# Batch 2's shared network behind the last mix, two thirds of batch 3's behind the expert loop

## The reference

```python
# x (4, 512, 512), ctx (4, 512, 256)
q = ctx @ Wq.T + bq;  k = ctx @ Wk.T + bk            # (4, 512, 128)
attention = softmax(q @ k.T, axis=-1)
x = x + tanh(g_xattn) * (layernorm(x) @ attention.T)
h = layernorm(x).reshape(-1, 512)
shared = (sigmoid(h @ shared_gate.T) * (h @ shared_up.T)) @ shared_down.T
weights = softmax(h @ router_w.T);  top_w, top_idx = top_k(weights, 2)
# routed: bfloat16, sum over the two chosen experts e of a token
routed = top_w * ((sigmoid(h @ w_gate[e].T) * (h @ w_up[e].T)) @ w_down[e].T)
x = x + tanh(g_ffn) * (h + shared + routed)
```

## Time and profile before

| what | us |
|---|---|
| median of three runs (lowest, highest) | 332.44 (330.88, 333.1) |
| the profiled execution | 332.47 |
| its span, first to last event | 330.7 |
| TensorE busy | 295.4 |
| VectorE, POOL, ScalarE busy | 216.4, 158.8, 132.0 |
| mean granted clock of TensorE | 0.973 of full |

### The profile page before, as it was taken

The page is one execution under the profiler, slowest core; times in us unless marked ns, Lnnn a source line. Parts: engine busy times, 40 slices in busy tenths (PEclk is TensorE's granted clock), DMA queues, the critical chain, the costliest instruction groups (busy, mean ns, idle before and its releaser), DMA issues.

```text
span 330.7 us, 6138 instructions
## 1 busy us (share of the span) xinstructions
PE 295.4 (89%) x1596; PEld 208.7 (63%) x1608; DVE 216.4 (65%) x585; ACT 132.0 (40%) x235; POOL 158.8 (48%) x238
## 2 busy tenths in 40 slices
PE   7579789999999999999999998799999999997280
PEld 2247658786878776877887786566666666663120
DVE  0788878478756588745467488576777676775291
ACT  2263577606657406678104370134343434342000
POOL 3706892685701757402767046035565555565100
PEclk9999989999999999999999999999999999999587
DMA  7999699022060120000159994333434334339499
GB/s 247 342 229 319 98 210 291 27 96 79 20 237 0 50 80 0 0 4 0 64 116 210 208 207 154 83 89 121 124 100 110 113 97 126 98 99 314 134 316 343
DMA packets 30612, 45.91 MB, mean 139 GB/s; under 512 B 3008, under 2 KB 20160, under 8 KB 30592
## 3 DMA queue, kind: packets, MB, share of 16 engines
q1 hardware_dynamic: 20016, 27.66, 27.5%
q0 software_dynamic: 10432, 17.99, 22.9%
q10 hardware_dynamic: 144, 0.00, 0.0%
HBM read 39.58 MB, written 14.72 MB: 164 GB/s over the span
## 4 chain that ended last, share of the span: by engine, by line
PE 68%; DMA 7%; DVE 7%; POOL 7%; issue 6%; ACT 2%; SPq 1%; POOLq 0%; DVEq 0%; ACTq 0%
PE bank L677 13%; PE bank L472 11%; PE bank L473 11%; PE bank L474 11%; PE bank L694 7%; POOL xg L398 5%; PE bank L484 4%; PE bank L467 4%; PE bank L669 3%; PE bank L685 2%; DMA z<-ysb,desti 2%; DMA zb<-z 2%; DMA wqk_sb<-wqk 1%; DVE acc L1272 1%; DVE prob L951 1%
## 5 line engine op out<-in xcount | busy, mean ns | idle before, releaser
L888 ACT ACTIVATE sigc<-bank 128x352 f32<-128x352 f32 x39 | 18.1, 463 | 67.0 <-PE bank L677 67.0
L451 POOL DMA_INDIRECT z<-ysb,desti x36 | 36.1, 1002 | 9.6 <-issue 9.3
L472 PE MATMUL bank<-lnT_hi,sgu_lo 128*128 128x512 f32 (+2 forms) x96 | 39.1, 407 | 1.6 <-DVE lnT_lo L988 1.6
L473 PE MATMUL bank<-lnT_lo,sgu_hi 128*128 128x512 f32 (+2 forms) x96 | 37.8, 394 | 0.0
L474 PE MATMUL bank<-lnT_hi,sgu_hi 128*128 128x512 f32 (+2 forms) x96 | 37.8, 394 | 0.0
L398 POOL DMA_INDIRECT xg<-lnb,slot x32 | 31.9, 996 | 9.9 <-issue 7.6
L1239 DVE TENSOR_TENSOR hrow<-sigc,bank 128x352 bf16<-128x352 f32 x39 | 20.3, 521 | 24.3 <-ACT sigc L888 16.9
L677 PE MATMUL bank<-wgu_lo,xTb 128*128 x156 | 36.0, 313 | 0.0
L677 PE MATMUL bank<-wgu_hi,xTb 128*128 x156 | 36.0, 312 | 0.0
L387 POOL TENSOR_TENSOR hT_lo<-sig,hT_hi 128x512 fp32r<-128x512 f32 (+1 forms) x9 | 11.6, 1289 | 45.7 <-ACT hT_hi L800 45.7
L1245 DVE TENSOR_SCALAR ysb<-bank,wt 128x512 bf16<-128x512 f32 x39 | 29.1, 747 | 5.7 <-DMA z<-ysb,desti 2.8
(11 more groups left out here) (178 smaller groups left out, 651.1 us busy)
## 6 DMA issues: line engine op xcount, KB each, us to landing
xt<-xg SPq DMA_DIRECT2D x39, 129.0 KB
xT_raw<-xT SPq DMA_DIRECT2D x4, 1024.0 KB, 7.3
acc<-x SPq DMA_DIRECT2D x4, 1024.0 KB, 9.5
out<-acc SPq DMA_DIRECT2D x16, 256.0 KB, 3.5
wgu_lo<-wguT POOLq DMA_DIRECT2D x2, 1408.0 KB, 13.3
wgu_hi<-wguT POOLq DMA_DIRECT2D x2, 1408.0 KB, 13.3
cx<-ctxT SPq DMA_DIRECT2D x4, 512.0 KB, 4.3
wd_sb<-wdT POOLq DMA_DIRECT2D x2, 1024.0 KB
```

Source lines behind the costliest of these rows:

```text
L451: nc.gpsimd.indirect_dma_start(out=z, out_offset=bass.IndirectOffsetOnAxis(ap=desti[:, r:r + 1], axis=0), in_=ysb[:, r, :], in_offset=None ...
L472: pe.matmul(dst, a_lo, b_hi, start=first, stop=False)
L473: pe.matmul(dst, a_hi, b_lo, start=False, stop=False)
L888: act.activation(sigc[:, v, :], bank[2 * v][:, 0:I], ACT.Sigmoid).then_inc(s["csig"], 1)
```

## The change

Batches 0 and 1 keep their order. For batches 2 and 3 each engine's list is written anew. On TensorE: project(3) and the energies of batch 3 are woven into mix(2); the turns of its softmax come earlier; mix(3) stands behind rank(2), in the middle of batch 2's shared network, whose rest and whose down product stand behind mix(3). Batch 3 gets only slice 0 of its shared network (with the logits) ahead of the loop; its lnT takes the space of probT. Slices 1 and 2 and the down product go behind the loop, the down product of a token tile into one bank with its two z rows. za and zb have room for all 16 tiles; zb is loaded in 8 pairs up front, and stores follow. tanh(g_ffn) is no longer in the routing weights but in the last addition. Buffers and banks are placed anew for it. wgu_hi and wd_sb are issued behind scatter(2) and factors2(3). The diff of the parts that the prediction speaks of:

```diff
+            for i in range(NB):
+                sp.dma_start(za[:, LT * i:LT * (i + 1)], zt[0, :, LT * i:LT * (i + 1)]).then_inc(s_za[i], 16)
+            sp.wait_ge(s["cy"], NE)
             for r in range(SLOTS):
                 sp.wait_ge(s_yd[r], 16 * len(range(r, NE, SLOTS)))
-
-            def store(t):
-                sp.wait_ge(s["comb"], t + 1)
+            for i in range(0, TT, 2):
+                sp.dma_start(zb[:, i:i + 2], zt[1, :, i:i + 2]).then_inc(s_zb[i // 2], 16)
+            for t in range(TT):
+                if t < LT * last_b:
+                    sp.wait_ge(s["comb"], t + 1)
+                else:
+                    sp.wait_ge(s["shared"], t + 1)
                 sp.dma_start(out[t * P:(t + 1) * P, :], acc[:, t, :]).then_inc(s["outd"], 16)
-            for t in range(TT):
-                if t >= ZS:
-                    store(t - ZS)
-                sp.dma_start(zb[:, t % ZS], zt[1, :, t]).then_inc(s_zl[t % ZS], 16)
-            for t in range(TT - ZS, TT):
-                store(t)
             sp.wait_ge(s["outd"], 16 * TT)
...
+            b = last_b - 1
+            x_low(last_b)
+            factors2(b)
+            factor1(last_b)
+            rows_copy(b)
+            scatter(b, 0)
+            scatter(b, 1)
+            factors2(last_b)
+
+            pool.wait_ge(s["eng"], TT)
+            pool.wait_ge(s["xmm"], TT)
+            for k in range(KP, NT):
+                pool.dma_start(wgu_hi[:, k - KP], wguT[:, k * P:(k + 1) * P, :].rearrange("e p i -> p e i")).then_inc(s["wgu2_in"], 16)
+            for k in range(IT):
+                pool.dma_start(wd_sb[0:KI[k], k], wdT[:, k * P:k * P + KI[k], :].rearrange("e p n -> p e n")).then_inc(s["wd_in"], 16)
+            rows_copy(last_b)
+            scatter(last_b, 0)
+            scatter(last_b, 1)
...
@@ -515,52 +554,71 @@
 
             def turn_ln2(b, j):
                 pe.wait_ge(s["ln2"], LT * b + j + 1)
-                if j >= 2:
+                if j >= 2 and b != last_b - 1:
                     pe.wait_ge(s["lnTlo"], LT * b + j - 1)
+                elif j >= 2:
+                    pe.wait_ge(s["lnTlo"], LT * b + j - 1)
+                elif b == last_b:
+                    pe.wait_ge(*((s["lgshift"], 2 * b), (s["place"], b))[j])
...
+                    pe.wait_ge(s_zb[t // 2], 16)
+                    pe.matmul(bank[6 + j % 2][:, :], identb[:], za[:, t, :], start=True, stop=False)
+                    pe.matmul(bank[6 + j % 2][:, :], identb[:], zb[:, t, :], start=False, stop=False)
                 for c in parts:
                     pe.wait_ge(s["hlo"], IT * b + c + 1)
                     k = ORDER[c]
                     m = KI[k]
                     mm = three(bank[6 + j % 2][:, :], hT_hi[0:m, k, tok], hT_lo[0:m, k, tok],
-                               sd_hi[0:m, k, :], sd_lo[0:m, k, :], c == 0, c == IT - 1)
+                               sd_hi[0:m, k, :], sd_lo[0:m, k, :], c == 0 and b < last_b, c == IT - 1)
                 if parts[-1] == IT - 1:
                     mm.then_inc(s["dm"], 1)
...
+            b = last_b - 1
+            project(last_b, 0)
+            project(last_b, 1)
+            mix(b, range(0, 1))
+            energy(last_b, 0)
+            energy(last_b, 1)
+            mix(b, range(1, 2))
+            energy(last_b, 2)
+            mix(b, range(2, 3))
+            energy(last_b, 3)
+            mix(b, range(3, 4))
+            down(b - 1, 0)
+            turn_prob(last_b, 0)
+            turn_prob(last_b, 1)
+            down(b - 1, 1)
+            turn_ln2(b, 0)
+            turn_ln2(b, 1)
+            down(b - 1, 2)
+            turn_ln2(b, 2)
+            turn_ln2(b, 3)
+            down(b - 1, 3)
+            wide_shared(b, 0, 1)
+            turn_prob(last_b, 2)
+            turn_prob(last_b, 3)
+            wide_shared(b, 0, 0, range(0, 2))
+            turn_logits(b)
+            wide_shared(b, 0, 0, range(2, NT))
+            wide_shared(b, 1, 0)
+            rank(b)
+            mix(last_b)
+            wide_shared(b, 1, 1, range(0, 2))
+            turn_ln2(last_b, 0)
+            turn_ln2(last_b, 1)
+            wide_shared(b, 1, 1, range(2, NT))
+            turn_ln2(last_b, 2)
+            turn_ln2(last_b, 3)
+            wide_shared(b, 2, 0)
+            wide_shared(last_b, 0, 1)
+            wide_shared(b, 2, 1, range(0, 2))
+            turn_logits(last_b)
+            wide_shared(b, 2, 1, range(2, NT))
+            wide_shared(last_b, 0, 0)
+            rank(last_b)
+            for j in range(LT):
+                down(b, j)
...
+            wide_shared(last_b, 1, 0)
+            wide_shared(last_b, 1, 1)
+            wide_shared(last_b, 2, 0)
+            pe.wait_ge(s["hid"], IT * last_b + 2)
+            for t in range(4):
+                routed(t)
+            wide_shared(last_b, 2, 1)
+            for t in range(4, 8):
+                routed(t)
+            down(last_b, 0)
+            for t in range(8, 10):
+                routed(t)
+            down(last_b, 1)
+            for t in range(10, 12):
+                routed(t)
+            down(last_b, 2)
+            down(last_b, 3)
 
...
+            b = last_b - 1
+            qk(last_b)
+            act.activation(warm[:], less_mean[:], ACT.Exp)
+            for j in range(LT):
+                soft(last_b, j)
+            for j in range(LT):
+                normalise(last_b, j)
+            prob_high(last_b, 0)
+            prob_high(last_b, 1)
+            x_high(last_b)
+            for j in range(LT):
+                ln2_high(b, j)
+            rows_again(b)
+            logits_out(b)
+            prob_high(last_b, 2)
+            prob_high(last_b, 3)
+            choice_exp(b)
+            gate_shared(b, 0)
+            for j in range(LT):
+                add_ln2(b, j)
+            hidden_high(b, 0)
+            gate_shared(b, 1)
+            ln2_high(last_b, 0)
+            ln2_high(last_b, 1)
+            hidden_high(b, 1)
+            ln2_high(last_b, 2)
+            ln2_high(last_b, 3)
+            gate_shared(b, 2)
+            rows_again(last_b)
+            logits_out(last_b)
+            act.activation(warm[:], less_mean[:], ACT.Exp)
+            hidden_high(b, 2)
+            choice_exp(last_b)
+            gate_shared(last_b, 0)
+            for j in range(LT):
+                add_ln2(last_b, j)
+            hidden_high(last_b, 0)
 
...
+            b = last_b - 1
+            qk_low(last_b)
+            residual(b, range(0, 1))
+            row_max(last_b, 0)
+            row_max(last_b, 1)
+            residual(b, range(1, 2))
+            row_max(last_b, 2)
+            over_sum(last_b, 0)
+            over_sum(last_b, 1)
+            residual(b, range(2, 3))
+            row_max(last_b, 3)
+            over_sum(last_b, 2)
+            over_sum(last_b, 3)
+            residual(b, range(3, 4))
+            ln2_apply(b)
+            prob_low(last_b, 0)
+            shared_out(b - 1, 0)
+            prob_low(last_b, 1)
+            ln2_low(b, 0)
+            shared_out(b - 1, 1)
+            ln2_low(b, 1)
+            ln2_low(b, 2)
+            shared_out(b - 1, 2)
+            ln2_low(b, 3)
+            shared_out(b - 1, 3)
+            prob_low(last_b, 2)
+            prob_low(last_b, 3)
+            choose(b)
+            weights(b)
+            places(b)
+            shared_hidden(b, 0)
+            residual(last_b, range(0, 2))
+            hidden_low(b, 0)
+            residual(last_b, range(2, LT))
+            ln2_apply(last_b)
+            shared_hidden(b, 1)
+            ln2_low(last_b, 0)
+            ln2_low(last_b, 1)
+            hidden_low(b, 1)
+            ln2_low(last_b, 2)
+            ln2_low(last_b, 3)
+            choose(last_b)
+            shared_hidden(b, 2)
+            hidden_low(b, 2)
+            weights(last_b)
+            places(last_b)
+            dve.wait_ge(s["rowsb"], NB)
+            dve.wait_ge(s["rowsb2"], NB)
+            tables_tiles()
+            tables_limits()
             tables_rows()
...
+            shared_hidden(last_b, 1)
+            for r in range(SLOTS):
+                dve.wait_ge(s_yd[r], 16 * len(range(r, NE, SLOTS)))
+            hidden_low(last_b, 1)
+            for t in range(4):
+                add_routed(t)
+            shared_hidden(last_b, 2)
+            add_routed(4)
+            add_routed(5)
+            hidden_low(last_b, 2)
+            for t in range(6, 8):
+                add_routed(t)
+            add_routed(8)
+            add_routed(9)
+            shared_out(last_b, 0)
+            add_routed(10)
+            add_routed(11)
+            shared_out(last_b, 1)
+            shared_out(last_b, 2)
+            shared_out(last_b, 3)
```

More of the change, by code:

```diff
@@ L537, in rank @@
                 sel = picked[:].rearrange("p j e -> p (j e)")
[L538 to L543 removed]
+                pe.matmul(rank_bank(b)[:, 0:LT * E], tri[:], sel, start=True, stop=True)
```

(5 more changed lines are left out.)

336 lines of the change are left out of this document (174 added, 162 removed).

## The result

The changed kernel takes 345.84 us (median of 4 runs, 344.86 to 347.6); the kernel before took 332.77 beside it (4 runs, 330.88 to 333.45). The ratio is 1.041, 95% interval 1.035 to 1.047: 13.1 us slower, where 13.2 was forecast. The profiled execution took 345.78 (span 344.0).

The account below looks back on a forecast made before the run. TensorE was taken as the bound, busy 295.4 of 330.7 us. Slots 4.6, clock 1.4, 1.7 and 2.1, and tail 3.4 sum to 13.2 on a median of 332.44: 345.7 us, range 340 to 353.

Parts of the forecast that it names:

- Step 1: Batch 2: TensorE idle 9.9 us before its first turn of lnr2, as rstd2 queues behind x_low(3) on POOL.
- Step 2: Batch 3: POOL and VectorE queues leave TensorE idle 3.4 and 1.4 us; its scatters start 4.6 us later.
- Step 3: Lower clock behind TensorE's idle times: 1.4 us after 9.9 idle, 1.7 after 3.4, 2.1 in the expert loop.
- the first wait: TensorE's idle time of 9.9 us in batch 2, with 1.4 us priced for the lower clock behind it.
- The weights: wgu_hi and wd_sb, issued later, all there at 211.0, ahead of the loop's start at 219.2: costed at nothing.
- Step 4: Tail behind the expert loop: 84 matmuls came and the gap holds 36, so 3.4 us longer.
- The rule weighed: x_low on POOL gets shorter with VectorE nearly idle: estimate 4.3 us, making the sum 345.4.

Follow-up runs that it names:

- e1: Changed kernel with x_low(3) on POOL behind factors2(2) and factor1(3) instead of ahead of them: 336.42 us, ratio 1.012 to the kernel before.
- e2: Changed kernel with x_high(3) on ScalarE ahead of batch 3's four normalisations instead of behind prob_high(3,1): 343.13 us, ratio 1.030 to the kernel before.
- e3: Changed kernel with all twelve matmuls of up product wide_shared(2,1,1) ahead of turn_ln2(3,0), not six ahead and six behind turn_ln2(3,1): 346.46 us, ratio 1.041.
- e5: Changed kernel with 24 and 26 matmuls on unread data filling TensorE's idle time ahead of the expert loop: 343.4 us, ratio 1.028 to the kernel before.
- e8: e3 with the two loads of wgu_hi issued on POOL ahead of batch 2's scatters instead of behind factors2(3): 346.3 us, ratio 1.043.
- e4: Changed kernel with one matmul instead of three in every product of batch 3 behind the expert loop: 341.64 us, ratio 1.027 to the kernel before.

## Why the prediction was right, step by step

**Step 1** held: the wait stood where the chain put it, 9.43 us for 9.9. x_low took 4.49 us for the 4.60 taken. e1 and e2 moved the turn by 8.0 and 3.7 us when the wait was taken away in whole and in part, and with the whole of it 7.5 of the 13.2 us at the end went.

**Step 2** held: the slots came 7.6 us later in the rows (201.25 against 193.63), for 4.6 + 1.4 + 1.7 = 7.7, and the places on the way held too: the first turn of batch 3's rows at 178.63 (177.2 and 1.4 of clock) and the third at 184.27 (181.0 and 3.1). e3 took 1.9 us of its idle time away and moved the slots by 0.7.

**Step 3** was right in what happens and a little off in a size: against the kernel before the loop lost 1.5 us to the clock, not 2.1; e5 gave back 1.7 in the loop. The 1.4 behind the first wait were there (0.50 in 144.34 to 148.00), but they are not the price of a long idle time: e1, with 1.42 and 0.63, paid them too.

**The weights** are the term that failed. They were all there when the prediction had them, at 211.6 (forecast 211.0), but "Costed at nothing; the scatters hide it" compared this with the loop's start. What counts is the scatters, which POOL issues behind them and which land behind them. From slots to the first wide product it took 19.19 us, not 17.87: 1.3 us, and e8 brought back 17.83. In e4, with the same order, it was 0.5, so that this size rests on single executions.

**Step 4** held, 0.5 too high: the tail is 2.85 us longer, not 3.4; e4 showed that its products make it so.

So 7.6 + 1.3 + 1.5 + 2.9 = 13.3 stands where 13.2 was forecast: a term of 1.3 that was missing and two that were 0.6 and 0.5 too large. That the total came within 0.1 is luck: these errors cancel.

The rule weighed: the Trainium skill, GPSIMD Engine Reference, section 8 (Key points), names contention between POOL and VectorE instructions with two SBUF inputs, and the prediction concluded that x_low gets shorter with VectorE idle. The rows show 4.49 us against a mean of 4.60, a change of 0.1, and not the 4.3 of the estimate from its section 2.1. That conclusion was not the page's: VectorE's instructions beside x_low at 131.40 all read an input from a bank, so none had two SBUF inputs.

## What to carry to other kernels

Before an instruction is put ahead on an in-order engine, write down what it waits for and what then queues behind it: one instruction of 4.5 us, put ahead of one of 1.0, cost 8 us. Work that moves into a gap was free up to the gap's length (8.17 us of it in 8.06), and the idle time that it left ahead of the loop was paid in clock until something filled it (e5, 1.7 us). For a transfer, compare its end with the next thing in its own queue, not only with its reader.
